# Experts' outputs weighed and added on VectorE, x weighed once per sequence, the whole convolution on VectorE, scan units taken in twos

## The reference

```python
h = tok_ref(x, ...)                                   # embedding * sqrt(192) + positions
h = h + attn_ref(layernorm(h), ...)                   # mixer + SwiGLU
h = h + ffn_ref(layernorm(h), ...)

# in attn_ref
zxbcdt = rmsnorm(x) @ in_proj_w
dt = softplus(zxbcdt[..., -24:] + dt_bias)
xBC = silu(causal_conv(xBC, conv_w, width 4) + conv_b)      # 512 channels
step: h = exp(dt * A) * h + (dt * xt) * bt ; y = h @ ct     # scan over 2048 tokens, 24 heads of 16, state 64
y = (ys + D * xh) * silu(z);  h = y @ out_proj_w
m = (silu(v @ w_gate) * (v @ w_up)) @ w_down,  v = rmsnorm(h)

# in ffn_ref: 8 experts of width 128, 2 chosen per token out of 2 of 4 groups, and a shared one
y = einsum('tei,edi,te->td', silu(x w1) * (x w3), w2, cw)   # cw is 0 for experts not chosen
return y + (silu(x sw1) * (x sw3)) @ sw2
```

## Time and profile before

| | us |
|---|---|
| median of 3 runs | 1049.33 (1046.11 to 1059.36) |
| the profiled execution, its own time | 1049.16 |
| its span, first to last instruction | 1047.3 |
| TensorE busy | 844.0 (81%) |
| VectorE busy | 632.7 (60%) |
| ScalarE busy | 621.1 (59%) |
| GpSimd busy | 506.9 (48%) |
| mean granted TensorE clock | 0.944 of full speed |

### The profile page before, as it was taken

The page is one execution under the profiler, slowest core; times in us unless marked ns, Lnnn a source line. Parts: engine busy times, 40 slices in busy tenths (PEclk is TensorE's granted clock), DMA queues, the critical chain, the costliest instruction groups (busy, mean ns, idle before and its releaser), DMA issues.

```text
span 1047.3 us, 23150 instructions
## 1 busy us (share of the span) xinstructions
PE 844.0 (81%) x7072; PEld 651.3 (62%) x7072; DVE 632.7 (60%) x1516; ACT 621.1 (59%) x1387; POOL 506.9 (48%) x812
## 2 busy tenths in 40 slices
PE   3464988887888888788888878888887888889867
PEld 2233676666667666566667656675665667667656
DVE  6456666757565675756566584655757565674623
ACT  3575565656756566666656656565656756566523
POOL 2353545655544454554445455443655544455513
PEclk9676999999999999999999989999999999999988
DMA  8200000000000000000000000000000000000000
GB/s 221 72 1 12 1 6 16 4 16 0 18 0 4 14 4 14 0 18 0 10 8 4 14 0 18 0 4 14 3 16 0 18 0 4 14 4 10 1 8 8
DMA packets 16468, 15.24 MB, mean 15 GB/s; under 512 B 6322, under 2 KB 15224, under 8 KB 16184
## 3 DMA queue, kind: packets, MB, share of 16 engines
q1 hardware_dynamic: 16440, 14.89, 5.4%
HBM read 10.69 MB, written 4.19 MB: 14 GB/s over the span
## 4 chain that ended last, share of the span: by engine, by line
issue 31%; PE 26%; POOL 21%; DVE 9%; ACT 6%; DMA 4%; POOLq 1%; SPq 1%; ACTq 0%; DVEq 0%
PE bank L1315 13%; POOL w_raw L566 8%; DMA tok<-tokens 4%; DVE mr L1052 3%; PE bank L1541 3%; PE bank L1475 2%; POOL xa L545 2%; POOL xw L466 2%; PE bank L1592 2%; PE bank L1504 1%; POOL state L479 1%; POOL w_raw L563 1%; PE bank L1455 1%; POOL t L484 1%; ACT er L734 1%
## 5 line engine op out<-in xcount | busy, mean ns | idle before, releaser
L566 POOL TENSOR_TENSOR w_raw<-w_raw 128x384 f32<-128x384 f32 x128 | 128.3, 1002 | 183.5 <-ACT w_raw L795 176.2
L1052 DVE SCALAR_TENSOR_TENSOR mr<-er,gm 128x512 f32<-128x512 f32 x192 | 147.1, 794 | 100.8 <-ACT er L734 100.7
L466 POOL TENSOR_TENSOR xw<-xd,er 128x64 f32<-128x64 f32 (+1 forms) x256 | 114.9, 472 | 131.1 <-ACT er L734 116.5
L1475 PE MATMUL bank<-mr,xd 128*32 128x128 f32 x1536 | 97.3, 289 | 52.6 <-DVE mr L1052 50.4
L734 ACT ACTIVATE er<-bank 128x512 f32<-128x512 f32 x192 | 110.0, 605 | 46.3 <-PE bank L1455 46.0
L1216 DVE TENSOR_TENSOR w_raw<-sg,bank 128x256 f32<-128x256 f32 x144 | 60.2, 420 | 104.8 <-ACT sg L806 103.8
L1592 PE MATMUL bank<-w2t,w_raw 128*128 128x192 f32 x576 | 122.8, 343 | 0.5 <-ACT w_raw L795 0.5
L806 ACT ACTIVATE sg<-bank 128x256 f32<-128x256 f32 x144 | 55.4, 385 | 112.9 <-PE bank L1315 112.7
L1315 PE MATMUL bank<-x_h,w_hi 128*128 128x256 f16 x288 | 82.8, 288 | 44.7 <-DVE w_raw L1216 44.5
L1475 PEld LDWEIGHTS bank<-mr,xd 128*32 128x32 f32 x1536 | 44.5, 110 | 110.7 <-DVE mr L1052 100.0
L1592 PEld LDWEIGHTS bank<-w2t,w_raw 128*128 128x128 f32 x576 | 96.4, 201 | 4.4 <-issue 1.1
(11 more groups left out here) (225 smaller groups left out, 2182.4 us busy)
## 6 DMA issues: line engine op xcount, KB each, us to landing
out<-w_raw SPq DMA_DIRECT2D x16, 192.0 KB, 2.0
w_raw<-weights SPq DMA_DIRECT2D x1, 1924.0 KB, 9.2
wt_raw<-weights SPq DMA_DIRECT2D x2, 962.0 KB, 14.8
pos<-position SPq DMA_DIRECT2D x16, 96.0 KB, 2.9
tok<-tokens SPq DMA_DIRECT2D x16, 70.0 KB
sums<-lj SPq DMA_DIRECT2D x16, 64.0 KB, 2.2
ri<-sums SPq DMA_DIRECT2D x64, 12.0 KB
w2t<-w SPq DMA_DIRECT2D x1, 864.0 KB, 19.4
```

The source lines that it names most:

```text
L466: ins = pool.tensor_tensor(xw[:, b].rearrange("p (g o d) -> p g o d", o=2, d=HD)[:, first // 2:first // 2 + n, odd, :], xd[:, b, h, odd * ...
L566: pool.tensor_tensor(acc[:], acc[:], wt_out[:, e % NWT], ALU.add).then_inc(acc_done, 1)
L1052: ve.scalar_tensor_tensor(mr[:, r % NER], er[:, r % NER], 1.0, gm[:, b, :].unsqueeze(1).to_broadcast([128, HG, Q]), ALU.min, ALU.mult)\
L1475: ins = pe.matmul(p_y[row:row + 32, k * Q:(k + 1) * Q], xd[:, b, h, :], mr[:, r % NER, heads.index(h), :], start=(h % 2 == 0), stop=(h % 2 ...
```

## The change

1. Experts' outputs: `weigh` on ScalarE and the additions on GpSimd go, with their buffers. VectorE does both at once, from PSUM (`weighed_sum`): one addition of h1 for expert 0, and for each of the others two multiply-adds of 192 columns into `acc`. The one for e - 3 stands behind `hh` of e. `down(e)` now waits for `out_sum`, as do `project_out` and the store.
2. x is weighed once per sequence: `running_sums` gets three more small products (`after16`), whose exponentials (`wend`) replace the last column of `er`. GpSimd's 8 instructions per sequence become one of 384 columns, and `er` no longer waits for GpSimd.
3. The convolution's last block is VectorE's too: blocks 0 and 1 ahead of the experts (6 taps instead of 3), block 2 in `route_groups`, none in `route_experts`, block 3 behind `hh` of expert 3.
4. Order: scan operands one expert earlier, silu of the convolution in two parts, `project_out` ahead of the first exponents. The scan goes in twos: two units' exponents, then two units' products.
5. ScalarE takes a silu of one column (`warm`) behind `split_v`, ahead of `skipped_x` (xk), so that a table load stands there.

```diff
+            def weighed_sum(c, e):
+                ve.wait_ge(ex_done, c * NX + e + 1)
+                if e == 0:
+                    if later(c):
+                        ve.wait_ge(out_written, c * 16)
+                    ve.tensor_tensor(acc[:], p_out[1][:, 0:NB * D].rearrange("p (b d) -> p b d", b=NB), h1[:], ALU.add)\
+                        .then_inc(out_sum, 1)
+                    return
+                if e == 1:
+                    ve.wait_ge(cw_ready, c + 1)
+                ve.wait_ge(out_sum, c * NX + e)
+                for b in range(NB):
+                    ins = ve.scalar_tensor_tensor(acc[:, b], p_out[(e + 1) % 2][:, b * D:(b + 1) * D], cw[:, b, e - 1:e],
+                                                  acc[:, b], ALU.mult, ALU.add)
+                ins.then_inc(out_sum, 1)
...
                     if p is not None:
+                        if e == 3:
+                            for k in range(1, KC):
+                                convolve_tap(p, NM - 1, k)
                         if e == 4:
                             operands(p)
-                        if e == 7:
+                        if e == 6:
                             scaled_x(p, 0)
                             scaled_x(p, 1)
-                        if e == 8:
+                        if e == 7:
                             masked_g(p)
+                    if e >= 3:
+                        weighed_sum(c, e - 3)
...
                     if e >= 2:
 
-                        pe.wait_ge(weighed, c * NX + e - 1)
+                        pe.wait_ge(out_sum, c * NX + e - 1)
...
                 if b is not None:
                     split_v(b)
+                    act.activation(warm[:], mhalf[:, 0:1], ACT.Silu)
                 if f is not None:
                     skipped_x(f)
...
             def body(p, f, b):
+                if b is not None:
+                    project_out(b)
                 if f is not None:
                     exponents(f, 0)
                     exponents(f, 1)
-                if b is not None:
-                    project_out(b)
...
-                for q in range(NQ):
-                    r = b * NQ + q
-                    if r + 2 < NR:
-                        exponents(c, r + 2)
-                    pe.wait_ge(m_ready, c * NR + r + 1)
...
+                for first in range(0, NQ, 2):
+                    for q in (first, first + 1):
+                        if b * NQ + q + 2 < NR:
+                            exponents(c, b * NQ + q + 2)
+                    for q in (first, first + 1):
+                        r = b * NQ + q
+                        pe.wait_ge(m_ready, c * NR + r + 1)
```

## The result

The changed kernel takes 1060.29 us, the median of four runs (1059.33 to 1061.76), against 1047.72 us for the kernel before in the same call (1041.75 to 1059.36): 1.0158 times as long, 95% interval 1.0113 to 1.0203. A second measurement gave 1060.15, 1.0068 times the kernel before of its call (1.0045 to 1.0092). So the change makes the kernel 0.7 to 1.6% slower, where 3.8% faster was forecast. The kernel before moves by about 1% between calls (medians 1046.5 to 1056.5), while the changed kernel came back at the same time within 0.2 us.

A forecast was written before the change was run, and what follows sets the result against it. TensorE, busiest at 81% but not full, was bound by its waits, mostly VectorE held up by GpSimd. Stages summed to 57.65, with half clock 58.15 against 61.04 us a body, giving 1008 us; range 984 to 1038.

The forecast's parts named there:

- GpSimd held the routing up: Routing on VectorE: without GpSimd's additions, taps and 32-column operations get shorter, 2.1 us in all.
- The new wait: Experts 3 to 8: TensorE waits 2.75 us at `down(2)` for expert 0's weighed sum on VectorE.
- The weighed add's size: Experts 3 to 8: a 192-column add on VectorE takes 0.33 us from start to start, 0.65 to 0.7 per expert.
- rivals 1: VectorE becomes the bound: weighed adds cost 0.43 us from start to start, half clock stays; 1036 us, chance 0.18.
- rival 4: Experts: TensorE waits for `out_sum` every round, adds at 0.62 us; slower than before, 1067 us, chance 0.06.
- Half clock, 0.5 a body: TensorE: half clock behind its longest wait, charged in one body of three, 0.5 us.
- Experts 3 to 8, 17.65: Stage 1: 14.1 us of TensorE's busy time plus waits of 2.75 and 0.8, against 15.44 before, a loss.
- they just pass: Experts 3 to 8: VectorE's chain of 1.55 us per round fits within a TensorE round of 1.74.
- Projection and scan of sequence 0, 10.1: Stage 2: 12.24 us less 2.1, from shorter `mr`, no wait for tokens, and scan by twos.
- Scan of sequence 1 to expert 2, 17.9: Stage 4: 20.53 us less 2.6, from faster routing (2.1) and `xw` leaving the scan (0.5).
- VectorE waits there for ScalarE's silu anyway: Ahead of `hh` of expert 0: three more taps on VectorE charged at nothing net.
- SwiGLU, 12.0: Stage 3: 12.44 us less 0.4; the 0.70 wait goes, but later `xk` delays `gt` some 0.3.

The follow-up runs named there:

- x1: Changed kernel with block 3's three taps moved from behind `hh` of expert 3 back into `route_experts`: 1039.28 us.
- x2: Changed kernel with each weighed sum one expert earlier (that of e - 2 in place of e - 3): 1019.68 us.
- w4: Changed kernel with the first two units' exponents ahead of the output projection, as before the change: 1058.05 us.
- w5: w4 with 40 products that nobody reads on TensorE ahead of `down(2)`: 1033.05 us.
- x4: Changed kernel with ScalarE's one-column silu, and so the table load, behind the instructions of `xk`: 1058.55 us.
- x6: Changed kernel with the edits of x1 and x2 together: 1007.39 us.
- x7: x6 with the edit of x4 added (`xk` ahead of `warm`): 1006.93 us.
- w1: Changed kernel with GpSimd's decay of the state cut to one of 24 heads per sequence: 1046.96 us.
- w3: x7 with exponents ahead of the projection, scan units one by one, and GpSimd's decay of sequence 1's state behind its addition of `xk`: 977.65 us.

## Why the prediction was wrong, point by point

**What held.** *GpSimd held the routing up.* From `hh` of expert 0 to that of expert 1 it is 2.98 us (439.82 to 442.80), where the kernel before took 5.37 (496.62 to 501.99), and each tap takes 0.48. The wait for expert 3's products is 0.69, forecast near 1. *The new wait.* 2.70 us at `down(2)`, forecast 2.75, with the queue that was named (x1 and x2 show it). The final one is 0.97 for 0.8. *The weighed add's size.* 0.74 a pair, with 0.41 for one alone, so rivals 1 and 4, which rest on 0.43 and 0.62 from start to start, did not come, though rival 4's 1067 lies near the measured time. The Trainium skill's rule on two SBUF inputs (SBUF — State Buffer, "Who interferes with whom") stands with the trace there. The drain that the Trainium skill gives for a table load (ScalarE: Activation LUTs, "What ACT_TABLE_LOAD costs") does not show, as forecast:

```profile
472.71 1.28 ACT L768 ACT_TABLE_LOAD   x1
474.00 0.20 ACT L768 ACTIVATE warm<-mhalf 128x1 f32<-128x1 f32 x1
474.11 1.29 ACT L628 ACTIVATE xk<-xs,dsk 128x256 f32<-128x256 f32 x3
```

The next activation starts 1.29 us after the load does. *The first two `mr`* take 1.29 us for 2.14, and *the tokens* are waited for no more.

**What failed.** The step that failed is the sum over the stages: all four came out longer than their terms, by 0.7, 0.9, 0.8 and 0.4 us, and half clock took 0.5 more than its term. The sum was 57.65 + 0.5 against 61.45 measured: 3.3 us a body, 46 us of the 52 between 1008 and 1060. The other 6 are outside the full bodies' period, which the forecast took at nothing: from the first `down` of the 14th full body to the end it is 124.6 us, and was 119.5. (The last step has a slip too: 1008.7, with a profiled execution 0.2 below the median, is 1009 and not 1008.)

1. *Half clock, 0.5 a body* ("I charge it in one body of three"): measured 1.03, the 1.41 and 0.65 of the two twin stages over two bodies. The reason given, that the longest wait is shorter than before, was no reason: 2.70 drew a stretch in every other body. Nor did the trace of before bear out one body in three: between 130 and 930 us, ten of its 13 experts' phases have a stretch, and the undisturbed one of the earlier trace rows is an exception. Its price was misread as well. The rows give 15.44 against 14.67, 0.77 us and not the 1.7 named, because slower products there fill what would be waits: TensorE is busy all of the 15.44. And a second stretch in the scan of sequence 1 was not looked for at all. The miss itself is 0.5 us; but x1, x2, w4 and w5 show that the half clock decides how much of any edit is kept.
2. *Experts 3 to 8, 17.65*: 18.33 at full clock, 0.7 more. The waits are the forecast ones (2.71 and 0.97 in that body). What was mis-sized is "they just pass": TensorE's busy time is 14.66 against the 14.1 taken. `down(3)` and `down(4)` start 1.98 and 1.82 us after the one before, where a round is 1.74. The first of them stands at 513.45, and the weighed sum of expert 1, which it waits for, ends at 513.30, so VectorE does not just pass there. The last eight products of the stage take 1.74 us, where they took 1.53 before. Together these are the 0.55.
3. *Projection and scan of sequence 0, 10.1*: 11.02. The first `mr` starts 3.35 us after the last `down` ends (466.37 against 463.02), forecast 3.1, and the fourth takes 1.02 for 0.69 under the decay; TensorE waits 0.59 for it, and `turn_v` stands behind those products. The forecast took `xw` away from the scan and did not ask what GpSimd does in the time that this leaves: its decay, which stays, now falls on another `mr`. The rest of the 0.9 is not traced to one instruction.
4. *Scan of sequence 1 to expert 2, 17.9*: 18.70 at full clock. With `xw` gone the decay starts at 491.53, under the `xn` pair and not behind it as before: the pair is 0.5 us longer, and TensorE waits 0.78 for it. The forecast had taken 0.5 here as a gain from `xw` going. And "VectorE waits there for ScalarE's silu anyway" does not hold for six taps:

```profile
499.33 2.96 DVE L922 SCALAR_TENSOR_TENSOR xa<-xr,cw_,xa 128x256 f32<-128x256 f32 x6
502.32 0.42 DVE L1144 TENSOR_TENSOR w_raw<-sg,bank 128x256 f32<-128x256 f32 x1
```

The silu of expert 0 ended at 502.00, and `hh` starts 0.32 later, straight behind the taps.

5. *SwiGLU, 12.0*: 12.38. The wait for `gt` stayed, 0.65 for 0.70; its cause changed from the table load to the later `xk`. The forecast named that chain and took 0.3 for it. x4 shows what was to be had: without the wait the stage takes 12.10, close to the 12.0, but only 1.7 of the 4 us arrived, with ten stretches in the experts for six.

What cost the change most is not a miss of the forecast. The queue ahead of `down(2)` was priced rightly and treated as the change's price, when it was only the order's: at 2.7 us a body it is what turns 3 to 4% faster (x2, x6) into slower. The forecast failed on the rest of the body, where each gain was taken at its best.

## What to carry to other kernels

When work moves to an in-order engine, list what stands ahead of the first result that somebody waits for, and put that result first: the same sums in another place of VectorE's order were worth 40.6 us. Where no engine is full, don't add the best case of each stage; each small overlap (a decay beside an `mr`, six taps beside a silu) gives 0.3 to 0.5 us back, and the two with the decay alone were worth 12 us here. Read the granted clock beside every wait, and when an edit brings nothing, compare the clock column before calling the edit useless (w4 and w5).

## What the runs showed of the hardware

- The half clock took back a whole edit. The exponents first gave 18.5 us on x7, whose waits are short, and 2.2 on the changed kernel, where stretches at 1.2 GHz went from 12 to 26; with TensorE kept busy in its wait of 2.7 us by products nobody reads, they went to 13 and 25.0 us came back. Filling the same wait in the changed kernel's own order gave 3.5: the six stretches in the experts went, and those in the scan rose from six to nine.
- Short waits can go with half clock too. In x7 no wait of TensorE in the 13 bodies is over 0.8 us, and it has six stretches, all in the scan of sequence 1; in w1, where the wait for `xn` is 0.28 for 0.78, that stage has none.
- In the changed kernel the stretches alternate: two bodies with the same two waits ahead of `down` (2.70 and 0.97, 2.71 and 0.97) run one at 0.91 and one at 1.00 in the experts (19.74 and 18.33 us). So the mean clock of a body is no property of its waits alone.
- A GpSimd multiply of 128x384 (0.84 us) stretches VectorE's `mr` from 0.69 to 1.02, and a pair of `TENSOR_SCALAR` with one SBUF input each from 0.67 to 1.17 (back to 0.67 in w1 and w3). So the slowing is not confined to instructions with two inputs in SBUF. By the Trainium skill (SBUF — State Buffer, "Who interferes with whom") `tensor_scalar` can run in a mode that takes the port pair shared with GpSimd; by that rule the trace agrees, and the forecast had told the rule for one SBUF input without this condition. The small 32-column `xw` beside the same pair in the kernel before left it at 0.67.
